# Second attention of a four-stage kernel: the first scores placed after two projections, and score operands made by VectorE instead of ScalarE and GpSimd

## The reference, cut to what matters

```python
q, k, v = (heads(layernorm(x) @ W.T + b) for W, b in ((Wq, bq), (Wk, bk), (Wv, bv)))   # 16 heads of 8
scores = einsum('bhqd,bhkd->bhqk', q, k) / sqrt(8)
scores = where(pos_q < pos_k, -inf, scores)
x = x + (softmax(scores) @ v) @ Wo.T + bo
```

## Time and profile before

| | us |
|---|---|
| median of 3 runs | 1322.91 (1320.02 to 1329.63) |
| profiled execution, its own time | 1315.67 |
| span of the profiled execution, first to last instruction | 1311.9 |
| busy in the span: PE, DVE, ACT, POOL | 1032.3, 801.5, 656.3, 881.3 |
| mean granted TensorE clock, share of 2.4 GHz | 0.874 |
| third stage: first projection product to last `q_aug` | 678.19 to 1001.97 |

### The profile page before, as it was taken

The page is one execution under the profiler, slowest core; times in us unless marked ns, Lnnn a source line. Parts: engine busy times, 40 slices in busy tenths (PEclk is TensorE's granted clock), DMA queues, the critical chain, the costliest instruction groups (busy, mean ns, idle before and its releaser), DMA issues.

```text
span 1311.9 us, 31369 instructions
## 1 busy us (share of the span) xinstructions
PE 1032.3 (79%) x11163; PEld 800.5 (61%) x11164; DVE 801.5 (61%) x1993; ACT 656.3 (50%) x1214; POOL 881.3 (67%) x1173
## 2 busy tenths in 40 slices
PE   2599999999999645999935789999998268999200
PEld 1467677676776435999923456666665258999200
DVE  3677878778777384555514567777664763655222
ACT  0266777676766301555524558777864004555100
POOL 0489999989989247555246889999763275553476
PEclk9899999999999756999955899999998558999655
DMA  9000000000000001232300000000000002323122
GB/s 241 1 2 2 2 11 10 2 11 10 2 10 10 16 18 29 72 76 78 57 24 21 19 17 24 23 23 14 9 10 17 24 15 63 79 74 68 54 78 76
DMA packets 56246, 45.70 MB, mean 35 GB/s; under 512 B 13570, under 2 KB 48258, under 8 KB 56130
## 3 DMA queue, kind: packets, MB, share of 16 engines
q0 software_dynamic: 9088, 18.63, 6.3%
q1 hardware_dynamic: 39378, 22.44, 6.1%
q10 hardware_dynamic: 7664, 3.04, 1.0%
HBM read 27.57 MB, written 16.52 MB: 34 GB/s over the span
## 4 chain that ended last, share of the span: by engine, by line
PE 61%; DVE 14%; POOL 11%; issue 4%; ACT 4%; DMA 3%; another core or an unknown queue 1%; ACTq 1%; DVEq 0%; POOLq 0%
PE PS L1645 11%; PE PS L1358 6%; POOL got L646 6%; PE PS L1427 5%; PE PS L1460 5%; PE PS L1360 5%; PE PS L1359 5%; PE PS L1409 3%; PE PS L1416 2%; PE PS L1440 2%; DMA b_cols<-in_L_ffn_b_dram 2%; PE PS L1610 2%; DVE M L851 2%; PE PS L1398 1%; PE PS L1402 1%
## 5 line engine op out<-in xcount | busy, mean ns | idle before, releaser
L545 POOL TENSOR_SCALAR_AFFINE_SELECT PT<-PT 128x256 f32<-128x256 f32 x512 | 221.3, 457 | 63.0 <-ACT PT L1155 61.4
L1155 ACT ACTIVATE PT<-PS 128x768 f32<-128x768 f32 x256 | 207.0, 809 | 107.9 <-PE PS L1555 56.4
L675 POOL DMA_INDIRECT xg<-normed,source x156 | 151.7, 973 | 115.1 <-PE PS L1623 77.7
L646 POOL DMA_INDIRECT got<-expert_rows,slot_of x128 | 122.5, 957 | 78.6 <-DMA expert_rows<-y_rows 46.4
L1284 ACT ACTIVATE hid<-PS,b_cols 128x256 f32<-128x256 f32 x312 | 122.6, 476 | 97.3 <-PE PS L1360 76.7
L1645 PE MATMUL PS<-W,hid 128*128 x1248 | 155.6, 279 | 2.4 <-issue 1.8
L1645 PEld LDWEIGHTS PS<-W,hid 128*128 128x128 f32 x1248 | 149.1, 195 | 3.8 <-issue 3.8
L1409 PE MATMUL PS<-causal_b,ident_b 128*128 128x256 bf16 x512 | 102.3, 284 | 25.3 <-DVE q_aug L924 12.5
L1427 PE MATMUL PS<-PT,v_aug 128*32 128x256 f32 (+1 forms) x2048 | 114.0, 342 | 5.9 <-POOL PT L545 5.8
L1358 PE MATMUL PS<-xg_hi,w_hi 128*128 128x256 f32 x312 | 96.9, 311 | 3.6 <-issue 3.5
L1114 DVE SCALAR_TENSOR_TENSOR X<-got,weight,X 128x128 f32<-128x128 f32 x128 | 50.0, 393 | 79.4 <-DMA got<-expert_rows,slot_of 70.7
(11 more groups left out here) (266 smaller groups left out, 3221.2 us busy)
## 6 DMA issues: line engine op xcount, KB each, us to landing
expert_rows<-y_rows SPq DMA_DIRECT2D x78, 128.0 KB
normed<-xn SPq DMA_DIRECT2D x16, 256.0 KB, 2.3
xg<-normed,source POOLq DMA_INDIRECT x156
W<-in_L_ffn_w_dram SPq DMA_DIRECT2D x1, 2048.0 KB, 15.5
got<-expert_rows,slot_of POOLq DMA_INDIRECT x128, 2.6
out_dram<-X SPq DMA_DIRECT2D x8, 256.0 KB
b_rows<-in_L_ffn_b_dram SPq DMA_DIRECT2D x2, 512.0 KB, 3.5
X<-in_L_attn_a_x_dram ACTq DMA_DIRECT2D x2, 256.0 KB, 4.7
```

Of the source, the lines that this page charges most:

```text
L545: ins = nc.gpsimd.affine_select(out=diagonal, in_=diagonal, pattern=[[0, 2], [1, P]], compare_op=ALU.is_ge, fill=0.0, base=0, channel_mult ...
L646: nc.gpsimd.indirect_dma_start(out=got[:, k, :], out_offset=None, in_=rows_out, in_offset=bass.IndirectOffsetOnAxis(ap=slot_of[:, which * ...
L675: nc.gpsimd.indirect_dma_start(out=xg[:, i % 4, b_, :], out_offset=None, in_=normed, in_offset=bass.IndirectOffsetOnAxis(ap=source[:, k:k ...
L1155: s.activation(PT[:, unit % 2, 2 * pair:2 * pair + 2, :], PS[:, 4:6, 0:3 * P], ACT.Exp).then_inc(m["exp_done"], 1)
```

## The change

- The prologue holds six steps: `prep`, `query` 0, `key` 0, `query` 1, `key` 1, `value`. The masks are written at the very start of PE's part, and `scores(0)` directly behind `key` 0.
- `query` 2 and 3 and `key` 2 and 3 of chunk 0 go into the early and late places of units 0 and 1; the steps of chunk 1 move accordingly, so that in chunk 0 six units hold two query or key steps each, and `value` of chunk 1 takes the early place of unit 7.
- A query or key step is read out by ACT once (`minus`), and DVE makes `qs` or `ks` from PSUM, the bias column and `minus` in one instruction. POOL's addition and ACT's `whole` are gone. Bank 7 is free when DVE's instruction is done, and scores wait for DVE.
- In a unit DVE takes the early step's operand ahead of `row_max(u+1)`, and the late step's behind it.
- POOL gathers three row tiles of chunk 1 ahead of the first root, and the other five behind it; DVE adds the first five in the prologue, three in unit 0. Statistics and root of chunk 1 move: the end of the statistics and the root from unit 0 to unit 1.

```diff
-        self.by_act = kind in ("query", "key", "query2", "out_t", "gate_t")
+        self.by_act = kind in by_act
...
-    FIRST = [("prep", 0, 7), ("query", 0, 6), ("key", 0, 5), ("value", 0, 4), ("query", 1, 7), ("key", 1, 6),
-             ("query", 2, 5), ("key", 2, 4), ("query", 3, 6), ("key", 3, 7)]
+    FIRST = [("prep", 0, 7), ("query", 0, 6), ("key", 0, 5), ("query", 1, 7), ("key", 1, 6), ("value", 0, 4)]
...
-    FIRST_EARLY = [None, None, ("query", 0), ("query", 1), ("query", 2), ("key", 2), ("query", 3), ("key", 3)]
-    FIRST_LATE = [None, ("prep", 0, 1), ("value", 0, 1), ("key", 0, 1), ("key", 1, 1), None, ("prep", 0, 2), None]
+    FIRST_EARLY = [("query", 2, 0), ("query", 3, 0), None, ("query", 0, 1), ("query", 1, 1), ("query", 2, 1), ("query", 3, 1), ("value", 0, 1)]
+    FIRST_LATE = [("key", 2, 0), ("key", 3, 0), ("prep", 0, 1), ("key", 0, 1), ("key", 1, 1), ("key", 2, 1), ("key", 3, 1), ("prep", 0, 2)]
...
-                    nc.gpsimd.tensor_tensor(dst[:, s.c % 2, s.g, :, :].rearrange("p b s -> p (b s)"), whole[:, which, :],
-                                            minus[:, which, :].bitcast(F32), ALU.add).then_inc(m["keys_ready" if which else "queries_ready"], 1)
+                gather_results("1", 1, range(0, 3))
                 root(m, 1)
+                gather_results("1", 1, range(3, 2 * CT))
...
+                elif s.kind in ("query", "key"):
+                    dve.wait_ge(m["queries_minus" if s.kind == "query" else "keys_minus"], s.stacked)
+                    v.scalar_tensor_tensor(dst[:, s.c % 2, s.g, :, :].rearrange("p b s -> p (b s)"), at, w["bias"][:, which, s.g:s.g + 1],
+                                           minus[:, which, :].bitcast(F32), ALU.add, ALU.add).then_inc(m["freed_dve"], 1)
...
+                    if plan.early[unit]:
+                        closing(m, w, plan.early[unit], False)
                     if unit + 1 < NCH * UNITS:
                         row_max(m, unit + 1, 3 * HD)
...
-                        s.activation(whole[:, which, :], at, ACT.Identity, bias=w["bias"][:, which, st.g:st.g + 1])
...
-                    pe.wait_ge(m["queries_ready"], plan.find("query", g, c).stacked)
-                    pe.wait_ge(m["keys_ready"], plan.find("key", g, c).stacked)
+                    pe.wait_ge(m["freed_dve"], max(plan.find("query", g, c).freed, plan.find("key", g, c).freed))
...
+                causal(range(4))
                 for s in plan.prologue:
                     step(s)
+                    if (s.kind, s.g) == ("key", 0):
+                        scores(0)
                 for s in plan.prologue[-4:]:
-                    if s.by_act:
-                        pe.wait_ge(m["freed_act"], s.freed)
-                    else:
-                        pe.wait_ge(m["freed_dve"], s.freed)
-                causal(range(4))
-                scores(0)
+                    pe.wait_ge(m["freed_dve"], s.freed)
```

More of the change, by code:

```diff
@@ L113, with __init__ @@
 class Step:
-    def __init__(self, kind, g, c, bank):
+    def __init__(self, kind, g, c, bank, by_act=("query", "key", "query2", "out_t", "gate_t")):
         self.kind, self.g, self.c, self.bank = kind, g, c, bank
-        self.by_act = kind in ("query", "key", "query2", "out_t", "gate_t")
+        self.by_act = kind in by_act
 def number(steps):
-    last, freed, kinds = {}, {True: 0, False: 0}, {}
+    last, freed, kinds, same = {}, {True: 0, False: 0}, {}, {}
     for k, s in enumerate(steps):
@@ L205, in __init__ @@
             c, u = divmod(unit, UNITS)
-            early, late = (self.EARLY[u], self.LATE[u]) if c else (self.FIRST_EARLY[u], self.FIRST_LATE[u])
+            early, late = ((*self.EARLY[u], 1), self.LATE[u]) if c else (self.FIRST_EARLY[u], self.FIRST_LATE[u])
             if unit == NCH * UNITS - 1:
                 late = ("turn", 0, 0)
-            self.early.append(Step(early[0], early[1], c + 1, 7) if early and c + 1 < NCH else None)
-            self.late.append(Step(late[0], late[1], c + late[2], 7) if late and 0 <= c + late[2] < NCH else None)
-        self.epilogue = [Step(k, g, NCH - 1 + dc, bank) for k, g, dc, bank in self.LAST]
+            for places, s in ((self.early, early), (self.late, late)):
+                places.append(Step(s[0], s[1], c + s[2], 7, self.BY_ACT) if s and 0 <= c + s[2] < NCH else None)
+        self.epilogue = [Step(k, g, NCH - 1 + dc, bank, self.BY_ACT) for k, g, dc, bank in self.LAST]
         in_cycles = itertools.chain(*zip(self.early, self.late))
@@ L606, in attention_b @@
             def attention_b():
-                m, w, plan = att_sems["b"], layers["b"], Plan()
-                def stack(s):
-                    dst, which = (qs, 0) if s.kind == "query" else (ks, 1)
-                    pool.wait_ge(m["freed_act"], s.freed)
-                    nc.gpsimd.tensor_tensor(dst[:, s.c % 2, s.g, :, :].rearrange("p b s -> p (b s)"), whole[:, which, :],
-                                            minus[:, which, :].bitcast(F32), ALU.add).then_inc(m["keys_ready" if which else "queries_ready"], 1)
-                root(m, 1)
-                for s in plan.prologue:
-                    if s.kind in ("query", "key"):
-                        stack(s)
-                    if s.kind == "query":
-                        gather_results("1", 1, range(2 * s.g, 2 * s.g + 2))
+                m, w = att_sems["b"], layers["b"]
+                gather_results("1", 1, range(0, 3))
+                root(m, 1)
+                gather_results("1", 1, range(3, 2 * CT))
                 for unit in range(NCH * UNITS):
                     c, u = divmod(unit, UNITS)
-                    for s in (plan.early[unit], None if c else plan.late[unit]):
-                        if s and s.kind in ("query", "key"):
-                            stack(s)
                     mask(m, unit, 0)
@@ L929, in attention_b @@
                 statistics(m, 0)
+                add_expert_rows("1", 1, range(0, 2), False)
+                adds = {("prep", 0): 2, ("query", 0): 3, ("key", 0): 4}
                 for s in plan.prologue:
                     closing(m, w, s, False)
-                row_max(m, 0, 3 * HD)
+                    if (s.kind, s.g) in adds:
+                        k = adds[s.kind, s.g]
+                        add_expert_rows("1", 1, range(k, k + 1), False)
+                    if (s.kind, s.g) == ("key", 0):
+                        row_max(m, 0, 3 * HD)
                 for unit in range(NCH * UNITS):
```

32 lines of the change are left out of this document (21 added, 11 removed).

## The result

The changed kernel takes **1336.38 us** (median of 8 runs, 1332.67 to 1345.47) against 1322.18 (1315.20 to 1329.63) for the kernel before: ratio **1.0112**, 95% interval 1.0078 to 1.0146, or 14 us slower. The profiled execution of the change took 1337.72 us.

What follows compares the result with a forecast made beforehand. The prediction took a ring through PE, ACT and DVE, no single engine, to pace steady units. It summed -12.3 (start), +3.1 (chunk 0) and +17.2 (chunks 1 to 6) to +8.0 us: 1331 on the median, range 1312 to 1342.

Steps and rivals of the forecast that it cites:

- the ring: Chunks 1 to 6: row maxima wait for DVE's operand, that for `minus`, that for early step; 39.0 us a chunk, +17.2.
- the start: Third stage up to its first `q_aug`: made at 689.9 instead of 702.24, a gain of 12.3 us.
- no change: Whole kernel: a difference below 1% (13.2 us), on the slow side, 1324 to 1338 us; chance 0.62.
- DVE's instruction: Operand made from PSUM, bias column and `minus`: taken as 0.69 us, at most 0.2 more.
- Chunk 0: The third stage's first chunk: 58 us instead of 54.91, between 55 and 61; +3.1 us.
- The two ends of the working: Chunk 0 summed from its units: 54.3 us at full clock, some 63 at half.
- bank 7's hold: Each query or key step in chunk 0 holds bank 7 for 2.54 us at full clock, 3.23 at half.
- chunk 0 stays at half clock: Rival: chunk 0 takes 63 us instead of 58, the whole 1336; chance 0.12, half of it beyond 1%.
- Chunk 1: Loses time to a late gather again, about 1 us beyond the ring: 39.9 us, +0.6.
- Chunk 7: Last chunk: makes no operands for another chunk and stays as it is.
- the third rival: The clock falls in the steady chunks: about 7 us a chunk; one chunk +15, two give 1345; chance 0.10.
- The sum: Whole kernel: -12.3 at the first `q_aug`, +3.1 in chunk 0, +17.2 in chunks 1 to 6: +8.0 us.

Runs made afterwards that it cites:

- PE filled: The change plus 112 additional 128x128 products that nobody reads, 16 of them ahead of chunk 1's `prep`; ratio 1.0048 against the kernel before.
- Without the wait for `minus`: The change, but for chunks 2 to 7 DVE's operand is projection plus bias alone and ACT's same-size instruction reads another tensor; one run, 1308.34 us.
- the new order and the old operands: The change's step order, but each operand made as before by two ACT readings and POOL's addition; ratio 0.9956 against the kernel before.
- old order and new operands: The kernel before, ten steps in the prologue, but DVE makes every operand from PSUM ahead of the row maxima, POOL adding nothing; ratio 1.0077.
- four kernels with the new order and these products: The change with additional products: DVE operands throughout, 1.0048; for chunk 0 alone, 0.9911; for chunks 0 and 1, 0.9883; that with products in chunk 1 too, 0.9855.

## Why the prediction was right, and where it was wrong

The range held and the sum had the right sign; the ring and the start were right in their mechanism. The time lies in the forecast's own 1324 to 1338 too, but no change is not what came: the change is 1.1% slower, clear of the noise, and slower by over 1% had a chance of 0.21. Three terms were too small: chunks 0, 1 and 7.

- **The start**: -12.3 forecast, -12.7 measured. Right. DVE's instruction took 0.75 where the prediction took 0.69; its upper end had that.
- **Chunk 0** failed as a size: "I take a little more than half of the way to full: 58". It took 65.41 at 0.56. The two ends of the working were good: 54.3 forecast at full clock, 53.55 measured with PE filled; 63 at half clock, 65.41 measured. Two steps in a unit were put at 5.08 and 6.46 at least; units 3 and 5 took 4.67 and 4.66 at full clock, 6.67 and 6.65 at half. The 4.67 is no breach of bank 7's hold: with PE filled, unit 3's early step had begun at 718.04, ahead of the `q_aug` at 719.52 from which the unit is read. At half clock units 1, 6 and 7 were put too low, at 6.46, 8.76 and 6.5; they took 7.43, 9.53 and 7.96, and in the last two PE was recorded busy all the time. The choice between the ends was the mistake. The prediction argued that more products in the same time would lift the clock; the clock fell instead, from 0.72 to 0.56, and what lowered it is open. That was the rival *chunk 0 stays at half clock*, with a chance of 0.12 and 1336 us as its time. That the median came out at 1336.38 is luck: the rival had neither the losses of chunks 1 and 7 nor the offset of the profiled executions, on which see the sum.
- **The ring**: right. 39.0 us forecast, 39.45 measured in chunks 2 to 4. The 0.45 is DVE's instruction: 840.41 to 841.08 is 0.67 from start to start, where the prediction had 0.61, in eight units 0.48. Chunks 5 and 6: +3.9 and +4.9 forecast, +4.1 and +4.7 measured. That POOL's lighter load saves nothing held: in chunk 6 POOL is busy 14.68 of 38.81 us.
- **Chunk 1**: +0.6 forecast, +2.6 measured, at a clock of 0.96. Without the wait for `minus` in it, chunk 1 took 36.81 at 1.00, 5.1 less. If the ring accounts for 3.95 of that, as in chunk 2, the rest was not taken apart. The ring need not be all of the loss against before: with the new order and the old operands, which have no such ring, chunk 1 took 41.16 at 0.92.
- **Chunk 7**: "stays as it is" failed by 3.8 us. Its first two units ran at 0.53 and 0.57, near half clock. This is the third rival in small, and it is not due to the new order alone (27.05 with the old operands). Unit 7 of chunk 6 and units 0 and 1 of chunk 7, in the change and then in the kernel with old order and new operands:

```profile
991.77:996.26 4.49, 3.18 (x41) 1.91 (x39) 3.39 (x12) 2.40 (x3) 2.18 (x6) 1.00 0.01 4
996.26:1002.14 5.88, 5.58 (x44) 3.43 (x42) 3.02 (x7) 2.02 (x3) 1.98 (x4) 0.53 0.00 0
1002.14:1007.62 5.48, 5.39 (x44) 3.11 (x42) 3.03 (x6) 1.76 (x4) 1.53 (x4) 0.57 0.01 3
```

```profile
990.44:994.95 4.51, 3.19 (x41) 1.91 (x39) 3.41 (x12) 2.40 (x3) 2.18 (x6) 1.00 0.01 4
994.95:998.75 3.80, 3.48 (x44) 2.14 (x42) 2.83 (x7) 1.96 (x3) 1.98 (x4) 1.00 0.00 0
```

  The unit ahead is the same to 0.02 us in both, and the clock fell in one and not in the other. But that other kernel lost clock elsewhere, in chunks 4 and 5, and the change with PE filled in chunk 0 lost it in chunk 4 and again in chunk 7 (30.80). Chunks 4 and 5 of the first, then chunk 4 of the second:

```profile
875.04:915.73 40.69, 36.65 (x378) 24.06 (x376) 31.27 (x73) 24.89 (x37) 23.82 (x45) 0.96 0.07 21
915.73:956.00 40.27, 36.23 (x377) 23.79 (x376) 28.90 (x65) 24.89 (x37) 16.51 (x38) 0.96 0.03 10
```

```profile
872.93:913.51 40.58, 36.55 (x378) 24.00 (x376) 31.31 (x73) 24.90 (x37) 23.91 (x45) 0.96 0.08 21
```

  So all three traces with the ring in every chunk have such a fall, and none of the other eleven has a chunk from 2 to 6 under 1.00 or a chunk 7 over 27.17. The rival's condition, more idle time of PE, was there (4.33 us in chunk 2 of the change, 1.62 before); which chunk it strikes is open.
- **The sum**: forecast +8.0. In the two profiled executions -12.7, +10.5, +2.6, +9.2, +4.1, +4.7 and +3.8 make +22.2, and their times differ by 22.05 (1337.72 and 1315.67); the 2.98 by which the stage began later were made up behind it. The medians differ by 14.2: the profiled execution of before was 6.5 below its median, that of the change 1.3 above. On the scale on which the sum was made, the forecast was thus short by 14 us; +22.2 on the median of 1322.91 would be 1345, outside the range. That the range held is in part luck. How much of the loss stands in the other executions of these two kernels can't be read; that chunk 0 is as long in all four traces of the new order, and chunk 7 in both traces with the new order and the ring, speaks against one odd execution.

## What to carry to other kernels

Before an operand moves onto an engine that is a link of the unit's ring, ask when its input is ready: a wait ahead of the link is paid in every unit, even on an engine that idles (here 0.38 to 0.59 us a unit in chunks 2 to 6, of the 0.81 that the wait holds). Steps that are moved out of a start into the first cycles are not hidden if those cycles run at half clock; price the stretch at both clock levels, and let the range reach the worse one. Even the level that the stretch showed before was too good a guess: 0.72 between the prediction's two ends would have been some 59 us, an estimate, and 0.56 and 65.41 us came. Products that nobody reads are a cheap test of whether half clock is the cause; in these runs they paid only where PE set the pace.

## What the runs showed of the hardware

- **PE recorded busy all the time and the clock still at half.** In units 6 and 7 of chunk 0 PE is busy 17.49 of 17.49 us at 0.50 and 0.51, while chunk 2 holds 1.00 with 35.12 of 39.45. So in these rows the busy share of the profile does not tell which of the two levels is granted. The Trainium skill (TensorE: Matmul & The Clock Gate, Part 1: The HAM clock gate) says that recent activity of the array lifts the clock. With 112 more products it rose to 1.00 in chunk 0, which agrees; in the two units, recorded busy throughout, it did not rise.
- **The same additional products did not always do the same.** In chunk 0 the clock was 1.00, 0.94, 0.88 and 0.88 in four kernels with the new order and these products.
- **DVE's operand took 0.06 us more than an addition of two tensors, and not for its third operand.** From PSUM, 128x512, two tensors took 0.69; the bias column with one tensor took 0.75 (L818 above), and with two 0.75 (L817). The column is the likely cause, but the operations differ too, and no run parts them.
